# Group 13's block made in fp32 with the late groups, the last group's x and sums in other buffers, and new costs and preferences of the planner, in a causal attention and routed FFN kernel

## The chip, the cores and the metric

One core of one Trainium2 chip runs the whole program. The metric is the device time of one execution in microseconds (us). PE is TensorE, PEld its weight loads, ACT ScalarE, DVE VectorE, POOL GpSimd, SP the engine that issues all DMAs here.

## The reference

Input x is (2, 4096, 256) in fp32. Attention has one head of 256 channels and a causal mask; then a router takes the 3072 of 4096 rows with the highest score, and these alone go through a 256x256 block and a GELU.

```python
q, k, v = split(x @ w_attn + b_attn)
a = softmax(q @ k.T / 16 + causal_mask) @ v
x = layernorm(x + a @ w_proj + b_proj)
score = x @ w_router
top = top_k(score, 3072)                # in each batch of 4096 rows
y = x; y[top] = gelu(x[top] @ w_block)
out = layernorm(x + y)
```

## The kernel before

**Tiling.** Each batch of 4096 rows is cut into 8 groups of 512 queries: groups 0 to 7 and 8 to 15. A group of number g in its batch has 4(g+1) key tiles of 128 rows: four on the diagonal, the others in pairs. An fp32 product is made as three fp32r products of high and low parts (`split3`, L535), so all operands are split into a rounded copy (high) and a rest (low). Since w_proj is folded into the values, "sums" are what the reference has after w_proj. The last channel of the values is replaced by ones, so its sum is the softmax's denominator.

**Stages of a group.** Projection (`project`): x transposed is loaded, split (L821 to L839), and multiplied with A and WV into `fbank[0]`. First product (`scores`, L535 into `sbank`, two banks in turn): one tile is six matmuls; ACT copies it into `ring` (L955), 34 slots of 512 columns; the last two tiles of all go to `xraw`. DVE keeps a running maximum (`running`, L980 to L1001). `row_max`: four transposes (L1030), a reduction and two small steps (L1040 to L1047), four transposes back (L1053). `softmax`, for each diagonal tile or pair: DVE subtracts the maximum (L1066), ACT takes the exponential (L1073) and the high part (L1080, `parts`, three slots), DVE the low part (L1085). Second product (`values`, L1128 to L1136): six matmuls for a tile of up to 512 queries, into the two `obank` banks; its values come by DMA into `vs`, six slots. A slot of `ring` is free when its tile's second product is done, so at most four tiles of a group can still be open when the last tile of the last group but those in `xraw` is copied. For groups with g of 3 and more the sums come out turned: ACT (for the last group DVE, L1206) copies them into `ot_sb` (L1194), PE turns them back (L1225), DVE divides by the denominator and adds the residual (`evac`, L1240, L1244), then statistics (L1251, L1256), roots on POOL (`istd`, L1155 on), router sums on DVE (L1354, for the last group L1373) and normalised rows x1 on ACT (`norm`, L1343).

**x and its residual.** `attention_out` loads the group's x (L1177) into `xres[:, G % 2]`, POOL adds the bias (L1186). The load of group G waits until group G-2 has stored its x1, taken its router sums and made its y (`g_y`, which POOL's add at L1556 signals).

**The block.** Groups below `LATE` with g of 3 and more take an "upright" way: the block is applied to the turned sums plus scaled x columns (`rows_scale` L1446, `rows_add` L1452, high and low parts L1456 and L1460, 24 matmuls of 128x256 by `split3` into `fbank`, GELU L1477). x1 and y go to DRAM and come back for the end. Groups from `LATE` on (14 and 15 before) keep x1 and y in `tail`, at home(u, n), where they are wanted at the end: PE transposes x1 (`pe_t`, L1490), ACT copies it (`fhi`, L1502) to `late_x`, PE multiplies in plain fp32 (`pe_f`, L1524, two pieces of two matmuls for each half of a group, eight records to a half), ACT takes the GELU (L1542), POOL adds x1 (L1556) after the last router score, DVE takes statistics (L1562, L1567), POOL the roots (`late_own`, `late_sums`, L1788 to L1808). `tail` lies over `xT`, so a late group's norm waits for the last scores and the last projection. Banks of the late fills are listed in `bank_no`; `freed` gives what each waits for.

**Dummies.** `busy` (L593) issues matmuls without use; `late_busy` does so after certain late fills:

```python
def late_busy(pe):
    pe.wait_ge(v_h, QT * len(groups))
    busy(pe, fbank[2][:, :], 2)
# at the end of pe_t(pe, j):
if late and G + j > LATE:
    late_busy(pe)
```

v_h counts the tiles that `evac` has finished, 4 for each group.

**The end.** `search(1)` finds the threshold of the second batch in eight rounds: DVE compares (L1668), PE counts (L1724), DVE sums and decides (L1679, L1685). Then `ties`, sixteen picks on DVE (L1917) between rows scaled for either outcome (ACT, L1902 and L1907), and sixteen stores of 256 KB. Pairs of rows below the late groups are loaded during the last second product, paced with its loads of values (`paced`, L1850, L1851).

**The order.** All instructions lie in named streams for each engine (`at`). `merged` rehearses each (its waits gathered, its cost from `COSTS`), and `planned` simulates the engines and fixes one order for each, by the critical way that an operation has ahead of it (`urgency`) plus the preference of its stream (`PREFER_US`), after a time margin (`MARGIN_US`). On the chip each engine runs its order strictly, and so does SP with its DMAs.

## Time and profile before

| | us |
|---|---|
| median of 3 runs | 961.22 |
| the three runs | 964.9, 961.22, 958.93 |
| span of the profiled execution | 962.9 |
| PE busy | 934.3 (97%) |
| DVE busy | 791.0 (82%) |
| ACT busy | 637.6 (66%) |
| POOL busy | 303.6 (32%) |

The profiled execution's own time isn't given apart from its span; the span lies within the three times. Times in the rows are us from the span's start, durations of single instructions are ns where marked. An idle time in square brackets is the engine's just before the row, with what ended it. The end that the timeline gives a matmul is modelled: consecutive rows of 0.39 us start 0.23 us apart, and the chain of waits shows the 0.23.

### The profile page before, as it was taken

The page shows a single profiled execution, that of the slowest core. Times are in us where ns is not written, and L with a number is a line of the kernel's source. Part 1 is how long each engine was busy: PE and PEld are TensorE (multiplying, and loading weights), DVE is VectorE, ACT ScalarE, POOL GpSimd, SP SyncE. Part 2 cuts the span into 40 slices and gives each one's busy share as a digit, 9 for nine tenths or more (in the row PEclk, how much of TensorE's full clock was granted, in tenths as well). Part 3 has the DMA queues.
Part 4 walks back from the last instruction along what each step waited for, and adds up shares of the span by engine and source line. Part 5 has one row for each costly group of instructions (what it writes and reads, how often), then busy time and mean ns, then how long its engine had stood idle before and what let it go on. Part 6 is the DMA issues. An engine that isn't in the chain of part 4 may idle for free.

```text
span 962.9 us, 15643 instructions
## 1 busy us (share of the span) xinstructions
PE 934.3 (97%) x5018; PEld 799.2 (83%) x5018; DVE 791.0 (82%) x1494; ACT 637.6 (66%) x1009; POOL 303.6 (32%) x460
## 2 busy tenths in 40 slices
PE   9999999999999999999999999999999999998892
PEld 7889988888888888888889998888888888887671
DVE  5789886967976885699989898999899789489768
ACT  4467665764873776486757757586689577449794
POOL 3423231333220335414541253314212422131162
PEclk9999999999999999999999999999999999999996
DMA  6535344454364365488533633535769635347734
GB/s 212 166 114 171 113 141 122 120 158 126 101 184 116 102 187 155 132 255 277 175 109 94 199 108 110 164 102 172 247 223 295 212 106 153 99 144 241 264 128 175
DMA packets 89044, 155.84 MB, mean 162 GB/s; under 512 B 8442, under 2 KB 18300, under 8 KB 88964
## 3 DMA queue, kind: packets, MB, share of 16 engines
q1 hardware_dynamic: 88964, 154.85, 51.5%
q8 instruction: 41, 0.67, 0.3%
q14 instruction: 39, 0.32, 0.1%
HBM read 114.96 MB, written 39.86 MB: 161 GB/s over the span
## 4 chain that ended last, share of the span: by engine, by line
PE 93%; DVE 3%; DMA 1%; ACT 1%; issue 1%; DVEq 0%; POOL 0%; SPq 0%; ACTq 0%
PE sbank L535 38%; PE fbank L535 13%; PE obank L1134 11%; PE obank L1136 11%; PE obank L1135 10%; PE obank L1128 2%; PE obank L1130 2%; PE obank L1129 2%; DMA vs<-v_scratch 1%; PE fbank L1225 1%; PE mbank L1053 1%; PE mbank L1030 1%; DVE tail L1917 1%; PE fbank L1490 1%; DMA xraw<-xt 0%
## 5 line engine op out<-in xcount | busy, mean ns | idle before, releaser
L535 PE MATMUL sbank<-qT,xT 128*128 128x512 f32 (+2 forms) x1728 | 411.5, 378 | 0.2 <-issue 0.2
L535 PEld LDWEIGHTS sbank<-qT,xT 128*128 128x128 f32 x1728 | 304.9, 188 | 52.8 <-issue 0.6
L955 ACT COPY ring<-sbank 128x512 f32<-128x512 f32 (+3 forms) x286 | 156.2, 548 | 179.4 <-PE sbank L535 132.0
L1085 DVE TENSOR_TENSOR ring_lo<-ring,parts 128x1024 fp32r<-128x1024 f32 (+4 forms) x175 | 174.4, 1007 | 21.9 <-ACT parts L1080 21.3
L1134 PE MATMUL obank<-ring_lo,vs 128*128 128x512 f32 x476 | 182.5, 383 | 7.4 <-issue 3.5
L1136 PE MATMUL obank<-parts,vs 128*128 128x512 f32 x480 | 183.2, 382 | 0.0
L1135 PE MATMUL obank<-parts,vs 128*128 128x512 f32 x480 | 182.9, 381 | 0.0
L1080 ACT CAST parts<-ring 128x1024 fp32r<-128x1024 f32 (+4 forms) x175 | 144.8, 834 | 45.5 <-PE obank L1136 35.8
L1066 DVE TENSOR_TENSOR ring<-ring,mbank 128x1024 f32<-128x1024 f32 (+4 forms) x175 | 158.2, 944 | 7.3 <-PE mbank L1053 7.2
L1073 ACT ACTIVATE ring<-ring 128x1024 f32<-128x1024 f32 (+4 forms) x175 | 142.6, 842 | 21.6 <-DVE ring L1066 21.2
L997 DVE TENSOR_TENSOR runmax<-ring,runmax 128x1024 f32<-128x1024 f32 x84 | 106.6, 1269 | 59.3 <-ACT ring L955 58.6
L1134 PEld LDWEIGHTS obank<-ring_lo,vs 128*128 128x128 f32 x476 | 90.4, 190 | 25.1 <-issue 6.7
L1556 POOL TENSOR_TENSOR yb<-xres,yb 128x512 f32<-128x512 f32 x28 | 41.0, 1481 | 210.6 <-ACT yb L1542 80.1
L1136 PEld LDWEIGHTS obank<-parts,vs 128*128 128x128 f32 x480 | 90.9, 189 | 17.0
L1135 PEld LDWEIGHTS obank<-parts,vs 128*128 128x128 f32 x480 | 91.2, 190 | 16.1
L1186 POOL TENSOR_TENSOR xres<-xres,b_tot 128x512 f32<-128x512 f32 x32 | 49.0, 1554 | 67.5 <-DMA xres<-x 66.1
L839 POOL TENSOR_TENSOR xT<-xraw,xT 128x512 fp32r<-128x512 f32 x27 | 38.4, 1436 | 78.0 <-ACT xT L821 77.0
L1452 POOL TENSOR_TENSOR ot_sb<-ot_sb,yb 128x512 f32<-128x512 f32 x16 | 22.5, 1405 | 98.5 <-PE fbank L1225 80.6
L992 DVE TENSOR_TENSOR runmax<-ring,runmax 128x512 f32<-128x512 f32 (+3 forms) x74 | 44.9, 606 | 9.7 <-ACT ring L955 8.5
L535 PEld LDWEIGHTS fbank<-WV,xT 128*128 128x128 f32 x384 | 49.8, 191 | 2.3 <-issue 0.3
L535 PE MATMUL fbank<-WV,xT 128*128 128x256 f32 x384 | 51.2, 283 | 0.0
L535 PE MATMUL fbank<-xT,A 128*128 128x512 f32 x192 | 49.4, 393 | 0.2 <-POOL xT L839 0.2
(244 smaller groups left out, 1257.7 us busy)
## 6 DMA issues: line engine op xcount, KB each, us to landing
vs<-v_scratch SPq DMA_DIRECT2D x288, 256.0 KB, 2.9
v_scratch<-vnew SPq DMA_DIRECT2D x30, 512.0 KB, 3.1
xres<-x SPq DMA_DIRECT2D x16, 512.0 KB, 4.0
out<-tail SPq DMA_DIRECT2D x32, 256.0 KB, 2.8
x_scratch<-xres SPq DMA_DIRECT2D x14, 512.0 KB, 3.0
y_scratch<-yb SPq DMA_DIRECT2D x14, 512.0 KB, 4.1
tail<-x_scratch SPq DMA_DIRECT2D x28, 256.0 KB, 3.4
tail<-y_scratch SPq DMA_DIRECT2D x28, 256.0 KB, 4.0
```

The lines of the kernel that those rows point to most:

```text
L535: mm = eng.matmul(o, lhs(lh, k), rhs(rh, k), start=n == 0, stop=n == len(todo) - 1)
L955: act.copy(slot(n)[:, c0:], sbank[n % NSS][:, c0:]).then_inc(a_copy, 1)
L992: dve.tensor_tensor(runmax[:, 0, c0:], slot(n)[:, c0:], runmax[:, 0, c0:], ALU.max).then_inc(v_max, 1)
L997: dve.tensor_tensor(runmax[:, :, :], slots(ns, 0), runmax[:, :, :], ALU.max).then_inc(v_max, 1)
L1066: dve.tensor_tensor(slots(ns, c0), slots(ns, c0), mbank[:, None, c0:].broadcast_to([P, len(ns), GQ - c0]), ALU.subtract).then_inc(v_z, 1)
L1073: act.activation(slots(ns, c0), slots(ns, c0), ACT.Exp, scale=SCALE).then_inc(a_exp, 1)
L1080: act.copy(hi_of(u), slots(ns, c0)).then_inc(a_hi, 1)
L1085: dve.tensor_tensor(slots_lo(ns, c0), slots(ns, c0), f32(hi_of(u)), ALU.subtract).then_inc(v_lo, 1)
L1134: pe.matmul(o, vh, lo_, start=i == 0, stop=False)
L1135: pe.matmul(o, vh, hi_, start=False, stop=False)
L1136: mm = pe.matmul(o, vl, hi_, start=False, stop=last)
L1186: pool.tensor_tensor(r[:, 2 * j:2 * j + 2], r[:, 2 * j:2 * j + 2], b_tot[:, None, :].broadcast_to([P, 2, C]), ALU.add).then_inc(g_xres, 1)
```

## The change

`LATE` goes from 14 to 13, so group 13 takes the late way. With it `late_x` is laid out for up to eight halves of high parts, `bank_no` of the late fills has twelve entries (5 and 6 are `obank`, 3 and 4 `sbank`), and the wait of `pe_f` for the last group's first reciprocal holds for groups 14 and 15 alone. The last group's sums go to `sbank` (`summed`), so its second product waits for all score copies, and `obank` is free once group 14's sums are copied. The last group's x is loaded to its place in `tail`; the load waits for the last scores and projection. The router product of the last group goes to `mbank`. `block_sums` waits for `v_btot`, and each late group's roots for those of the late group before. The planner gets other costs, a model of a slowed PE after idle time, and new preferences and margins for nearly all streams.

```diff
-LATE = 2 * (T // GQ) - 2
+LATE = 2 * (T // GQ) - 3
+IDLE_US, SLOW_US = 1.3, 3.5
-PREFER_US = {"ffn flo": 100, "final load": 100, "project vhi": 100, "ffn store": 100, "last chain": 60,
...
+PREFER_US = {"final_roots own": 506, "project vhi": 455, "last": 412, "project qlo": 384, "scores copy": 369,
...
-MARGIN_US = {"attention_out router": 3, "final scale": 3, "project xhi": 2, "ffn flo": 2, "final_roots": 2,
...
+MARGIN_US = {"final own": 5, "attention_out norm": 5, "final sums": 3, "ffn sums": 3, "final_roots own": 3,
...
-COSTS = {"pe": (.0, 1 / 2400, .2), "act": (.13, 1 / 1200, .14), "dve": (.09, 1 / 960, .12),
-         "pool": (.35, 1 / 460, .1), "sp": (.45, 0.0, 0.0)}
+COSTS = {"pe": (.0, 1 / 2383, .2), "act": (.075, 1 / 1200, .17), "dve": (.065, 1 / 960, .13),
+         "pool": (.1, 1 / 445, .18), "sp": (.45, 0.0, 0.0)}
...
-        time = r.time * (COLD if n in COLD_STREAMS or e == "pe" and when < COLD_US else 1.0)
+        if e == "pe" and when > 2 * COLD_US and when - free[e] > IDLE_US:
+            slow = when + SLOW_US
+        time = r.time * (COLD if n in COLD_STREAMS or e == "pe" and when < slow else 1.0)
...
-        bank_no[f] = (3, 4, 5, 3, 4, 5, 6, 3)[4 * (G - LATE) + 2 * j + (kind == "ff")]
+        bank_no[f] = (5, 6, 5, 6, 5, 6, 5, 3, 4, 5, 6, 3)[4 * (G - LATE) + 2 * j + (kind == "ff")]
...
-                if bank_no[f] == 6:
-                    eng.wait_ge(v_ot, CC)
-                    eng.wait_ge(v_ow, 1)
-                elif bank_no[f] == 5:
-                    eng.wait_ge(v_ot, 1)
+                if bank_no[f] >= 5:
+                    eng.wait_ge(a_ot, CC * turned(len(groups) - 1))
                 elif bank_no[f] >= 3:
-                    eng.wait_ge(a_copy, n_tiles)
+                    eng.wait_ge(v_ot, bank_no[f] - 2)
...
-        last_ow = obank[1][:, 0:QT]
+        last_ow = mbank[:, 160:160 + QT]
+        summed = lambda G: sbank if G == len(groups) - 1 else obank
...
+                pe.wait_ge(v_btot, 1)
                 for k in range(CC):
...
-                    if G and straight(G - 1):
+                    if G == len(groups) - 1:
+                        pe.wait_ge(a_copy, n_tiles)
+                    elif G and straight(G - 1):
...
-                    o = obank[c][:, c0:]
+                    o = summed(G)[c][:, c0:]
...
+            if G == len(groups) - 1:
+                r = flat[:, (NUT - 2) * 512:NUT * 512].rearrange("p (t c) -> p t c", t=QT)
...
-                if G >= 2:
+                if G == len(groups) - 1:
+                    sp.wait_ge(p_s, n_tiles)
+                    filled(sp, ("v", G, 1))
+                elif G >= 2:
...
-                if late and 0 in tiles_:
+                if G >= len(groups) - 2 and 0 in tiles_:
                     pe.wait_ge(v_rs, 2 * len(groups) - 1)
...
-                    pool.wait_ge(g_own, 1)
+                if G > LATE:
+                    pool.wait_ge(g_own, G - LATE)
```

## Rows read from the trace of the kernel before

**Rows 1.** The page: busy time of each engine.
```profile
PE 934.3 (97%) x5018; PEld 799.2 (83%) x5018; DVE 791.0 (82%) x1494; ACT 637.6 (66%) x1009; POOL 303.6 (32%) x460
```

**Rows 2.** Busy time by stretch: length, PE, PEld, DVE, ACT, POOL, clock, DMA share, GB/s.
```profile
10.00:858.97 848.97, 847.92 (x4591) 732.51 (x4590) 704.80 (x1283) 559.11 (x879) 269.87 (x368) 1.00 0.51 157
858.97:869.81 10.84, 10.84 (x69) 9.43 (x67) 8.85 (x18) 4.98 (x10) 0.00 (x0) 1.00 0.64 197
869.81:923.97 54.16, 47.12 (x202) 38.47 (x203) 43.36 (x76) 45.11 (x65) 12.23 (x19) 0.94 0.79 267
923.97:931.34 7.37, 7.08 (x49) 5.97 (x48) 5.52 (x24) 7.04 (x14) 4.03 (x13) 1.00 0.00 1
931.34:949.35 18.01, 13.10 (x80) 7.76 (x78) 15.22 (x70) 16.50 (x38) 10.56 (x21) 0.90 0.01 1
949.35:962.90 13.55, 0.00 (x0) 0.00 (x0) 9.85 (x16) 2.08 (x4) 1.42 (x7) 0.50 0.83 310
...
870.00:880.00 10.00, 7.17 (x32) 6.16 (x33) 10.00 (x11) 9.98 (x13) 0.00 (x0) 0.88 0.63 226
```

**Rows 3.** Timeline of PE, 871 to 877: start, duration, instruction, idle before.
```profile
871.42 0.47 PE L1134 MATMUL obank<-ring_lo,vs 128*128 128x512 f32 x1 [1.61 <-ACT ot_sb L1194]
...
876.97 0.47 PE L1134 MATMUL obank<-ring_lo,vs 128*128 128x512 f32 x1 [1.41 <-ACT parts L1080]
```

**Rows 4.** Timeline of PE, 895 to 901.
```profile
895.18 0.47 PE L1134 MATMUL obank<-ring_lo,vs 128*128 128x512 f32 x1 [0.50 <-DMA vs<-v_scratch]
...
900.33 0.47 PE L1134 MATMUL obank<-ring_lo,vs 128*128 128x512 f32 x1 [3.52 <-issue]
```

**Rows 5.** The chain that ended last, 863 to 883: start, duration, what.
```profile
863.76 1.42 PE fbank L535 x12
...
870.21 1.06 ACT ot_sb L1194 x2
...
879.38 0.43 PE obank L1134
...
882.22 0.23 PE obank L1134
```

**Rows 6.** Timeline of DVE, 895 to 903.
```profile
895.77 1.49 DVE L1373 CUSTOM_DVE_ANT_0 runmax<-xres,wr 128x256 f32<-128x256 f32 x1 [4.25 <-POOL xres L1186]
...
897.44 0.43 DVE L1373 CUSTOM_DVE_ANT_0 runmax<-xres,wr 128x256 f32<-128x256 f32 x1 [0.17 <-DVE mcol L1373]
...
899.00 3.49 DVE L1085 TENSOR_TENSOR ring_lo<-ring,parts 128x1024 fp32r<-128x1024 f32 x3
```

**Rows 7.** Timeline of SP: the issue of the last load of x.
```profile
886.15 0.38 SPq L1177 DMA_DIRECT2D xres<-x  x1
```

**Rows 8.** Timeline of POOL, 881 to 897.
```profile
881.43 2.55 POOL L1556 TENSOR_TENSOR yb<-xres,yb 128x512 f32<-128x512 f32 x2 [22.62 <-issue]
894.45 2.53 POOL L1186 TENSOR_TENSOR xres<-xres,b_tot 128x512 f32<-128x512 f32 x2 [10.47 <-DMA xres<-x]
```

**Rows 9.** DMA queue, 894 to 898: packets, MB, share of the 16 engines.
```profile
q1 hardware_dynamic: 775, 1.41, 99.8%
```

**Rows 10.** Timeline of DVE, 860 to 862.
```profile
860.13 1.28 DVE L1460 TENSOR_TENSOR x1p<-ot_sb,vnew_b 128x512 fp32r<-128x512 f32 x2
```

**Rows 11.** Timeline of PE behind the last second product: fp32 blocks.
```profile
925.51 1.99 PE L1524 MATMUL sbank<-runmax,late_x 128*128 128x256 f32 x8
...
930.40 1.97 PE L1524 MATMUL sbank<-runmax,late_x 128*128 128x256 f32 x8 [0.29 <-issue]
```

**Rows 12.** Timeline of DVE, 932 to 940: count reductions, y statistics.
```profile
932.96 0.29 DVE L1679 TENSOR_REDUCE mbank<-fbank 128x15 f32<-128x120 f32 x1 [0.30 <-PE fbank L1724]
...
934.76 0.29 DVE L1679 TENSOR_REDUCE mbank<-fbank 128x15 f32<-128x120 f32 x1 [0.42 <-PE fbank L1724]
...
937.14 0.29 DVE L1679 TENSOR_REDUCE mbank<-fbank 128x15 f32<-128x120 f32 x1 [0.99 <-PE fbank L1724]
...
938.45 0.74 DVE L1562 BATCH_NORM_STATS2 bnst<-tail 128x6 f32<-128x256 f32 x2
```

48 lines of the change are left out of this document (30 added, 18 removed).

## The prediction

> **What bounds the kernel now.** I read the page first for the busy shares: PE is busy 934.3 us of the 962.9 us span [rows 1], so only what PE waits for, and what stands in front of it and behind it, can be won. Then I cut the span into stretches where the work changes [rows 2]. Of the 28.6 us in which PE idles, the stretches shown hold 26.8 us, so 1.8 us lie in the first 10. From 10 to 859 it idles 848.97 - 847.92 = 1.05 us in all, at full clock: a new order of instructions has next to nothing to win there and much to lose. From 859 to 869.8 (last scores, last row maxima, the held-back end of group 14's second product) it idles nothing. The second product of the last group, 869.8 to 924.0, holds PE busy for 47.1 of 54.2 us at a mean clock of 0.94: the 7.04 us idle and the slow clock are the loss to be had. From 924.0 to 931.3 the last chain makes the last scores of the router, from 931.3 to 949.4 DVE searches for the threshold, then sixteen picks and their stores follow, with DMA 0.83 busy. In these last three stretches PE isn't the bound; DVE is.
>
> The timeline of PE names the waits inside the product: 1.61 us for ACT's copy of group 14's sums, 1.41 us for the first pair's high parts [rows 3], 0.50 us for a load of values and 3.52 us put down to "issue" [rows 4]. Sum 7.04 us, all of the idle time. After the second and the fourth, the chain shows matmuls of 0.43 us in place of 0.23 [rows 5], eight each time, so 2 x 8 x 0.20 = 3.2 us more: the engine had been idle 3.0 us within 7 us, or 3.5 us at once, and the granted clock fell to 1.2 GHz. Loss in the product: 7.0 + 3.2 = 10.2 us.
>
> What is behind "issue"? DVE works in order. It stands 4.25 us in front of the last group's router sums (L1373), which wait for POOL's residual [rows 6], which starts at 894.45, 8.3 us after the load of x was issued at 886.15 [rows 7, 8]. The low parts that PE wants are queued behind at 899.00. And the load could go no earlier: it overwrites group 13's buffer, which POOL's add at L1556 reads until 884.0 [rows 8].
>
> **The change part by part.** The sum is made against the profiled execution: its span is 962.9 us; what lies around the span isn't shown, and the median of the runs is 961.2, so I take 1.7 us off at the end.
>
> Sums of the last group in sbank. The first values matmul of group 15 waits for its score copies (done before 860) and no longer for the ot copy. The 1.61 us wait goes. What is late next is ACT: it is busy 9.98 of the 10 us from 870 to 880 [rows 2], and the second wait (1.41 us) is for its high parts. But ACT's two ot copies (1.06 us on the chain [rows 5]) may now come after the exponentials, and with group 13's gelus late, four activations and two table loads leave that stretch of ACT. I expect both waits, 3.0 us, to shrink to about 1. Bounds: 0, and 3.0 if the idle time only moves from the first wait to the second.
>
> x of the last group in the tail. Its load now waits for the last scores and the last projection, both over by 860.5, not for 884.0. So x and the residual are there some 20 us before DVE asks. The 4.25 us wait of DVE goes and with it PE's 3.52 us. The four router sums (3.2 us of DVE, less with POOL gone) stay and have to lie where PE has low parts in stock. Bounds of the gain: 0 to 3.52 us, plus the clock; I take all.
> The price: the residual moves to where DVE makes the first low parts. The first router sum beside it took 1.49 us, its sisters 0.43 us [rows 6]. So two residual adds of 1.27 us can each hold up DVE by 1.1 us: 0 to 2.2 us, I take 0.5. That is a reason against the early x, in the same bounds.
>
> Loads. The product runs 0.79 of the DMA engines busy; between 894 and 898 they are at 99.8% [rows 9]. If PE waits less, the same values and paced loads are wanted in less time. Against that, group 13's x1 and y no longer go to DRAM and back, 2 MB, and its paced pairs are gone. I leave 1.0 us of waits for values (0.50 now; bounds 0 to 4). For the clock I leave 1.0 us of the 3.2, for a bout that is half as long.
> Left over in the product: 1.0 + 0.5 + 1.0 + 1.0 = 3.5 us. Gain: 10.2 - 3.5 = 6.7 us.
>
> Group 13's block in fp32. Out: 24 matmuls, 2 x 1.42 us [rows 5], at 863.8 to 868.4, and DVE's two low parts, 1.28 us, between the last maxima [rows 10]; rows, sums, their scaling and adding lie under PE's work and cost nothing. In: transposes 0.44 us and an fp32 block of 1.88 us for each half. Not all of it gets behind the second product, though. The second half's transposes end with late_busy, whose wait on v_h is for the last group's residual sums. One rehearsed operation takes all its waits together, and the real wait blocks what is queued behind. So only the first half (0.44 + 1.88 = 2.3 us) can be done behind the product, and the second half, with all of group 14, comes after 928. In 863 to 924 PE is relieved of 2.84 and given 2.3: gain 0.5 us. This holds if something covers the place from which 2.84 us go. PE has 6.9 us there (four held-back tiles of six matmuls of 0.23 us, and the last projection, twelve matmuls like those of 1.42 us [rows 5]), and the row maxima come 1.3 us or more earlier without the low parts, so the first values should be ready as the held-back ones end. If they aren't, up to 2.84 us of idle time appear: bound of loss.
>
> Behind the product. Before, group 14's first block (925.5) stood ahead of the router product, but DVE's own steps up to the aggregates last as long, so its going gives 0.1 us at most. After it PE made three more, the first at 930.4 [rows 11]; now it makes five, the first before the last score. One such block stretched a round of the search: reduction to reduction 2.38 us against 1.80, 0.6 us [rows 12]. Two more in this stretch, with their transposes: 1.0 us; bounds 0 (all of it in the gaps) and 4.6 us (all in the path). Two more pairs of y statistics on DVE (0.74 us each) fill the wait for a count, which is 0.42 us where nothing fills it [rows 12]: about 0.25 each, 0.5. POOL's two more adds (1.27 each) and one more chain of roots (eight small steps, by my estimate no longer than two such adds and a half) end before 958, when the pick of the last pairs needs them. Cost behind the product: 1.0 + 0.5 - 0.1 = 1.4 us.
>
> Planner's costs and preferences. They change the order of all five queues. Where PE idles 1.05 us in 849, I cost this at 0, with -1 as one end; the other end is open and is the third rival. The waits added at block_sums and in the roots of late groups lie on steps done long before: 0.
>
> Sum: 962.9 - 6.7 - 0.5 + 1.4 = 957.1 us of span, 955.4 us as a median.
>
> **The rivals.** (1) Nothing is left over in the product, and the new order hides the additional blocks: 962.9 - 10.2 - 0.5 + 0.3 = 952.5, with 1 us found in the head 951.5; median 949.8. For it: the waits have two named causes and both are cut; ACT and DVE have 9 and 11 us free in the product. Against: the first pair's way (exp, high, low) is serial, and DMA is near full.
> (2) The waits move. Loads of values now end the wait where x did (5.1 us kept), and 2.3 us of idle time open where group 13's block was cover: 962.9 - 10.2 + 5.1 + 2.3 + 1.4 = 961.5; median 959.8. For it: 99.8% DMA at the worst place; held-back values are limited to four tiles by the ring. Against: 2 MB less traffic.
> (3) Slower. The new order puts on DVE, in each group, an instruction that waits for a DMA or POOL ahead of the low parts, as L1373 did. The place is the second batch, where DVE is busiest. The price of one is that of 894 to 904: 3.52 + 1.6 = 5.1 us. From two such stalls on (10.2 against a gain of 5.8) the kernel is slower; with three it is 962.9 - 5.8 + 15.3 = 972.4, median 970.7. For it: such a stall is in the present order; large preferences overrule urgency. Against: only one in 963 us, and the present costs were cruder.
> (4) That the block isn't behind the product at all, its first half too coming after it: the 2.3 us change sides and the sum is within 1 us of the forecast.
>
> **How the numbers follow.** Forecast (with 4) 0.44, rival 1 0.26, rival 2 0.19, rival 3 0.11. About 1% (9.6 us) is what a measurement of this kernel tells from no change, as its three runs lie 6 us apart. Faster by over 1% means below 951.6: rival 1, 0.26. Slower by over 1%: rival 3 where it reaches three stalls, 0.10. Between: 0.64. The range of 8 in 10 runs from 948.5 (rival 1 with a little of the head) to 961.5 (rival 2 and a little more).
>
> **What would show it.** Right: no wait of PE for ot_sb; the load of x issued soon after 860, no DVE wait at the router sums; the product's stretch about 50 us (54.2 before) with under 3 us idle; one group of 8 fp32 matmuls for group 13 before the last values, the second after the last residual sums; five blocks behind; 18 to 19.5 us from last score to first pick. Wrong: PE idle between 20 and 859 of more than 2 us, or a product still as long with waits for vs, or a search of 21 us and more.

## The result, and the profile after

The changed kernel takes 977.46 us in the median of four runs (977.35 to 978.36); the kernel before, on the same chip, takes 962.55. The ratio is 1.0167, with a 95% interval of 1.0141 to 1.0194, all of it above 1: slower by 1.7%. The profiled run took 977.35 us with a span of 975.6, 12.7 us over the 962.9 of before. The prediction, 955.4 with a range up to 961.5, was wrong.

The stretches say where. These are the busy times of the changed kernel's stretches, in the columns of [rows 2], cut at the same events: start of the last second product (called "the product" from here on), its end, last score, first pick. The last row is a stretch of its own:
```profile
10.00:883.50 873.50, 859.44 (x4634) 739.30 (x4632) 707.36 (x1293) 552.49 (x879) 284.64 (x372) 1.00 0.48 153
883.50:929.94 46.44, 45.63 (x217) 38.09 (x217) 41.35 (x71) 46.37 (x71) 3.08 (x9) 1.00 0.84 284
929.94:937.28 7.34, 5.00 (x32) 3.57 (x31) 5.52 (x23) 7.32 (x15) 1.20 (x2) 0.76 0.00 0
937.28:962.13 24.85, 19.95 (x111) 13.65 (x109) 17.79 (x78) 14.98 (x31) 16.94 (x38) 0.91 0.00 1
962.13:975.60 13.47, 0.00 (x0) 0.00 (x0) 9.79 (x18) 3.97 (x8) 2.38 (x8) 0.50 0.84 311
...
700.00:800.00 100.00, 91.26 (x439) 74.80 (x438) 76.22 (x135) 61.76 (x101) 32.03 (x39) 0.98 0.64 208
```
Against [rows 2]: the product starts 883.5 - 869.8 = 13.7 us later; it is 54.2 - 46.4 = 7.7 us shorter; from its end to the first pick it is 32.2 against 25.4 us, 6.8 more; the picks take the same. 13.7 - 7.7 + 6.8 = 12.8, which is the difference.

**Ahead of the product.** From 10 us on PE idles 873.50 - 859.44 = 14.06 us there, where it had idled 1.05. 8.74 us of them lie between 700 and 800, the second batch, where the kernel before has PE busy for all of the 100 us. PE's timeline there has 0.55 + 2.46 + 1.35 = 4.4 us of waits for ACT's copies of scores, 2.42 for a row maximum of DVE, and 1.87 for POOL's xT. The timeline of ACT, 722 to 729, and under it that of PE, show how one of these waits comes about:
```profile
722.50 0.59 ACT L970 COPY ring<-sbank 128x512 f32<-128x512 f32 x1
726.23 1.09 ACT L1888 ACTIVATE tail<-tail,coef 128x256 f32<-128x256 f32 x2 [3.14 <-DMA tail<-y_scratch]
727.23 0.56 ACT L970 COPY ring<-sbank 128x512 f32<-128x512 f32 x1
...
722.36 3.03 PE L547 MATMUL sbank<-qT,xT 128*128 128x512 f32 x12 [0.55 <-ACT ring L970]
727.84 2.03 PE L547 MATMUL sbank<-qT,xT 128*128 128x512 f32 x6 [2.46 <-ACT ring L970]
729.67 0.63 PE L1151 MATMUL obank<-ring_lo,vs 128*128 128x512 f32 x1
```
ACT works in order. At 723.1 its next instruction is a scaling (L1888) of the first batch's final rows, work that nobody waits for soon; but its operand is still being loaded. The copy of scores (L970) that empties a bank for PE is queued behind it. ACT stands 3.14 us, PE 2.46, and the matmuls that follow take 0.63 us where their like took 0.39 just before: the granted clock went down to half. By groups of waits (total, times, longest), of the changed kernel and then of the kernel before:
```profile
ACT tail L1888 <- DMA tail<-y_scratch: 19.4, 6, 5.8
```
```profile
ACT tail L1907 <- DMA tail<-y_scratch: 1.1, 1, 1.1
ACT tail L1864 <- DMA tail<-y_scratch: 1.0, 1, 1.0
```

**In the product.** The load of x is issued at 877.17, 6.3 us ahead of the product's start (before, 886.15 [rows 7], 16.3 us behind it), and the residual is done before DVE asks; of PE's four waits [rows 3, 4] one of 0.81 us is left; the clock stays at 1.00. Timelines of SP, POOL and PE, and DVE's first router sum, which waits for nothing and takes 0.42 us in place of 1.49 [rows 6]:
```profile
877.17 0.38 SPq L1200 DMA_DIRECT2D tail<-x  x1
881.11 2.56 POOL L1209 TENSOR_TENSOR tail<-tail,b_tot 128x512 f32<-128x512 f32 x2 [42.17 <-DMA tail<-x]
884.31 0.47 PE L1151 MATMUL sbank<-ring_lo,vs 128*128 128x512 f32 x1 [0.81 <-ACT parts L1095]
913.83 0.42 DVE L1396 CUSTOM_DVE_ANT_0 runmax<-tail,wr 128x256 f32<-128x256 f32 x1
```

**Behind it.** The last score is there at 937.28. Timeline of PE, then DVE's first reductions of counts:
```profile
936.56 3.78 PE L1547 MATMUL obank<-runmax,late_x 128*128 128x256 f32 x8 [1.38 <-ACT late_x L1525]
941.65 0.22 PE L1747 MATMUL fbank<-cmp,ones_bf 128*128 128x120 bf16 x1
...
941.90 0.29 DVE L1702 TENSOR_REDUCE mbank<-fbank 128x15 f32<-128x120 f32 x1 [2.31 <-PE fbank L1747]
944.79 0.26 DVE L1702 TENSOR_REDUCE mbank<-fbank 128x15 f32<-128x120 f32 x1
```
The fp32 block of group 13's second half comes at 936.56, after the last residual sums, and at half clock: 3.78 us where [rows 11] have 1.97. The first count's matmul stands behind it, and behind the dummies and the four transposes of the next half, so the first reduction comes 4.6 us after the last score, where before it came 1.6 us after it (932.96 [rows 12] against 931.34).

PE's order sets these 3.0 us, since the comparison that the count wants is done at 939.30. A smaller delay stands behind it. Ahead of the comparison DVE turns the scores into keys, an operation of 128x8. In the changed kernel POOL's first addition of y, which waited for the last score, runs beside it; before, none did. Timelines of POOL and DVE in the changed kernel, and of DVE before:
```profile
937.43 1.26 POOL L1579 TENSOR_TENSOR tail<-tail 128x512 f32<-128x512 f32 x1 [1.04 <-DVE score L1415]
937.72 1.00 DVE L1668 TENSOR_SCALAR keyi<-keyi 128x8 uint32<-128x8 uint32 x1
```
```profile
931.82 0.17 DVE L1645 TENSOR_SCALAR keyi<-keyi 128x8 uint32<-128x8 uint32 x1
```
DVE takes 1.00 us for eight columns, where it took 0.17, and is done as POOL's addition ends. It takes 0.96 to 1.00 us in all fourteen kernels of this document where such an addition runs beside it, and 0.17 in the three where none does (before, e3_buffers, e13_before_tuned). As long as PE is late this costs nothing more; with PE out of the way it does (e8_countfirst below).

From the first of the eight reductions to the last it takes 17.4 us instead of 14.0 (941.90 to 959.33; 932.96 to 947.00).

### The profile page after: what moved, and what is told of

It is laid out like the page before. It is cut to its first block, busy times and chain, and to the rows that moved or that the text cites. A ratio compares the mean times of both kernels' runs of the same rounds, so it can differ in the third digit from the quotient of the medians.

```text
span 975.6 us, 15627 instructions
## 1 busy us (share of the span) xinstructions
PE 938.8 (96%) x5022; PEld 800.2 (82%) x5022; DVE 784.7 (80%) x1490; ACT 628.1 (64%) x1003; POOL 313.7 (32%) x462
## 4 chain that ended last, share of the span: by engine, by line
PE 76%; issue 6%; DVE 6%; DMA 5%; POOL 3%; ACT 2%; SPq 1%; DVEq 0%; ACTq 0%; POOLq 0%
PE sbank L547 31%; PE fbank L547 10%; PE obank L1151 8%; PE obank L1153 8%; PE obank L1152 8%; DMA out<-tail 2%; PE obank L1145 1%; PE obank L1146 1%; PE obank L1147 1%; PE sbank L1151 1%; PE sbank L1153 1%; PE sbank L1152 1%; DVE ring_lo L1100 1%; DMA tail<-y_scratch 1%; DMA ring<-xt 1%
## 5 line engine op out<-in xcount | busy, mean ns | idle before, releaser
L970 ACT COPY ring<-sbank 128x512 f32<-128x512 f32 (+3 forms) x286 | 157.1, 551 | 174.9 <-PE sbank L547 122.8
L1151 PE MATMUL obank<-ring_lo,vs 128*128 128x512 f32 (+3 forms) x416 | 159.1, 382 | 0.8 <-ACT parts L1095 0.8
L1153 PE MATMUL obank<-parts,vs 128*128 128x512 f32 (+3 forms) x416 | 157.8, 379 | 0.0
L1152 PE MATMUL obank<-parts,vs 128*128 128x512 f32 (+3 forms) x416 | 157.7, 379 | 0.0
L1153 PEld LDWEIGHTS obank<-parts,vs 128*128 128x128 f32 x416 | 78.5, 189 | 14.7
L1151 PEld LDWEIGHTS obank<-ring_lo,vs 128*128 128x128 f32 x416 | 78.6, 189 | 14.5 <-ACT parts L1095 1.0
L1152 PEld LDWEIGHTS obank<-parts,vs 128*128 128x128 f32 x416 | 78.6, 189 | 13.5
L1475 POOL TENSOR_TENSOR ot_sb<-ot_sb,yb 128x512 f32<-128x512 f32 x14 | 24.9, 1782 | 160.8 <-DVE yb L1469 150.6
L854 POOL TENSOR_TENSOR xT<-xraw,xT 128x512 fp32r<-128x512 f32 x27 | 40.5, 1515 | 66.6 <-ACT xT L836 65.7
L1209 POOL TENSOR_TENSOR xres<-xres,b_tot 128x512 f32<-128x512 f32 x30 | 44.8, 1518 | 51.9 <-DMA xres<-x 50.6
L1579 POOL TENSOR_TENSOR yb<-xres,yb 128x512 f32<-128x512 f32 x26 | 37.5, 1460 | 60.3 <-ACT yb L1565 27.6
L1172 POOL TENSOR_SCALAR roots<-mv_h 128x4 f32<-128x4 f32 x15 | 7.8, 519 | 151.3 <-DVE mv_h L1279 125.8
```

The lines of the kernel that those rows point to most:

```text
L854: pool.tensor_tensor(xT[:, 1, k, cols], raw_of(G)[:, k, :], f32(xT[:, 0, k, cols]), ALU.subtract).then_inc(g_xlo, 1)
L970: act.copy(slot(n)[:, c0:], sbank[n % NSS][:, c0:]).then_inc(a_copy, 1)
L1151: pe.matmul(o, vh, lo_, start=i == 0, stop=False)
L1152: pe.matmul(o, vh, hi_, start=False, stop=False)
L1153: mm = pe.matmul(o, vl, hi_, start=False, stop=last)
L1209: pool.tensor_tensor(r[:, 2 * j:2 * j + 2], r[:, 2 * j:2 * j + 2], b_tot[:, None, :].broadcast_to([P, 2, C]), ALU.add).then_inc(g_xres, 1)
```

## Experiments

Each time stands against runs of the kernel before on the same chip (medians 961.45, 960.48, 960.90, 961.47 and 961.01 for the five sets below). "Idle ahead" is PE's from 10 us to the start of the last product.

**1. Orders and structure apart.** e1_newplan is the kernel before with the changed planner alone: its costs, its idle rule, and its PREFER_US and MARGIN_US.
```
+IDLE_US, SLOW_US = 1.3, 3.5
...
-COSTS = {"pe": (.0, 1 / 2400, .2), "act": (.13, 1 / 1200, .14), "dve": (.09, 1 / 960, .12),
-         "pool": (.35, 1 / 460, .1), "sp": (.45, 0.0, 0.0)}
+COSTS = {"pe": (.0, 1 / 2383, .2), "act": (.075, 1 / 1200, .17), "dve": (.065, 1 / 960, .13),
+         "pool": (.1, 1 / 445, .18), "sp": (.45, 0.0, 0.0)}
```

> The kernel before with the planner's new costs, model, preferences and margins alone. Theory (the new order makes the loss): PE idles 8 us or more between 10 and the start of the last product (1.05 before, 14.1 in the changed kernel), and the time is 970 to 977. Rival (the late form of group 13 and the new buffers make it, the order only follows them): under 3 us idle there, 958 to 964.

Measured: 990.46 us, ratio 1.0303 (1.0285 to 1.032), 13 us above even the range of the theory. The planner's numbers alone cost 29 us, and the buffers have no part in it:
```profile
10.00:888.80 878.80, 867.29 (x4658) 747.28 (x4656) 717.00 (x1305) 557.90 (x888) 289.24 (x380) 0.99 0.50 155
```
11.5 us idle ahead, and a start 19 us late. From the product's end (942.12) to the first pick (974.20) it takes 32.1 us, 6.7 more than before, without any additional block there.

e2_oldplan is the reverse: the changed kernel with COSTS, PREFER_US and MARGIN_US of before, and without the new idle rule. e3_buffers is the buffers alone, with the block left early and the old planner:
```
-LATE = 2 * (T // GQ) - 3
+LATE = 2 * (T // GQ) - 2
```

> The changed kernel with the planner's old costs, preferences and margins. Theory (order): under 3 us idle before the last product, the product shorter by 6 to 8 us than before, the stretch behind it longer by 2 to 7, so 955 to 963. Rival (structure): 8 us or more idle, 970 and more.

> The old plan and only two late groups, but the last group's sums and x in the other buffers. Theory (the product's gain comes from the early x and the early start, the loss behind it from group 13's two more blocks): the wait of 3.5 us and that of 1.6 us are gone, the stretch behind the product stays at 39 us, 953 to 957. Rival (the gain hangs on the new order): the product keeps its 54 us, 960 to 963.

Measured: e2_oldplan 976.60 us, 1.0153 (1.0135 to 1.017); e3_buffers 981.78, 1.0212 (1.0192 to 1.0232). Both miss the theory's ranges, 955 to 963 and 953 to 957; e2_oldplan has the rival's time (970 and more) without its 8 us of idle time, and e3_buffers lies above its rival's 960 to 963 too. Ahead of the product, first e2_oldplan, then e3_buffers:
```profile
10.00:871.30 861.30, 857.69 (x4637) 740.84 (x4635) 707.20 (x1266) 559.04 (x877) 264.20 (x356) 1.00 0.50 155
```
```profile
10.00:867.00 857.00, 855.59 (x4635) 739.27 (x4633) 708.79 (x1270) 558.81 (x876) 266.76 (x356) 1.00 0.50 157
```
The middle is nearly whole again (3.6 us idle in e2_oldplan, 1.4 in e3_buffers). The product is no shorter than before: 55.4 us in e2_oldplan, and 55.3 in e3_buffers, whose last matmul of it ends at 922.3, with the early block's 24 matmuls inside it; PE then waits 5.1 us until DVE copies the last sums at 929.30. PE, DVE and ACT of e2_oldplan:
```profile
873.69 0.67 PE L1136 MATMUL sbank<-ring_lo,vs 128*128 128x512 f32 x1 [2.43 <-issue]
884.10 0.76 PE L1136 MATMUL sbank<-ring_lo,vs 128*128 128x512 f32 x1 [4.84 <-ACT parts L1080]
...
871.04 1.47 DVE L1381 CUSTOM_DVE_ANT_0 runmax<-tail,wr 128x256 f32<-128x256 f32 x1 [1.32 <-POOL tail L1194]
...
877.65 1.09 ACT L1916 ACTIVATE tail<-tail,fin 128x256 f32<-128x256 f32 x2 [0.77 <-DMA tail<-y_scratch]
```
The old preferences, with x there early, put a router sum in front of the first low part: that is the way to the wait of 2.43 us. The larger one, 4.84, has nothing to do with x: ACT makes four scalings of final rows, from 877.65 on, ahead of the first pair's exponential, and DVE five subtractions ahead of its low part. So the early x buys nothing by itself; it needs an order that puts its readers, and the scalings, later. The four kernels stand at 961.5 (before, old planner), 990.5 (before, new), 976.6 (changed, old) and 977.5 (changed, new): each half of the change loses with the other half missing, and the two together lose as well. The 1.47 us beside POOL's residual are [rows 6]' 1.49 once more.

Most of what these two lose lies behind the product: 5.1 us more to the first pick in e2_oldplan and 14.1 in e3_buffers, and in both 4.5 more in the picks, 18.0 us against 13.5 (e7_oldpref_dma28 and e10_gate below have the same). There DVE takes the last statistics of y only behind fourteen picks, and the last two picks then wait for POOL's roots and ACT's scalings; of e2_oldplan:
```profile
970.95 0.73 DVE L1926 COPY_PREDICATED tail<-mbank,tail 128x512 f32<-128x512 uint32 x1 [4.31 <-ACT tail L1916]
```

**2. The scalings in the middle.** e4_scale_margin is the changed kernel with one number changed, so that the planner keeps a scaling back until 3 us after its operand is due:
```
-             "final scale": 0.3, "ffn flo": 0.3, "proj": 0.3, "scores": 0.3, "ffn fhi": 0.3}
+             "final scale": 3, "ffn flo": 0.3, "proj": 0.3, "scores": 0.3, "ffn fhi": 0.3}
```

> The changed kernel with the margin of the stream final scale back at 3 us (0.3 in the change). Theory (ACT stands in front of the first batch's scalings, whose rows haven't landed, with score copies queued behind): the 14.7 us that ACT waits for tail between 700 and 800 shrink under 4, PE's 8.7 us idle there shrink under 3, and the time is 966 to 970. Rival (PE is starved there by the whole order, and the waits are slack): 975 to 979.

Measured: 972.01 us, 1.0135 (1.0091 to 1.0178).
```profile
700.00:800.00 100.00, 96.32 (x484) 80.79 (x483) 80.98 (x141) 68.23 (x114) 34.74 (x40) 1.00 0.68 220
ACT tail L1888 <- DMA tail<-y_scratch: 9.5, 5, 4.1
```
ACT's waits for these loads are halved, PE's idle time from 700 to 800 falls from 8.74 to 3.68 us, and 5.4 us of the time go: the mechanism is shown, as one cause of several (9.6 us idle ahead are left). The theory had expected more of it: waits under 4 us, PE's idle time under 3, and 966 to 970 us.

e6_dma28 (the changed kernel, planner's latency of a transfer 2.8 us instead of 2.0) and e7_oldpref_dma28 (that, with the preferences and margins of before) ask whether the planner just believes in too quick a load:
```
-DMA_US, DMA_BYTES_US, FIRST_BYTES_US = 2.0, 320e3, 250e3
+DMA_US, DMA_BYTES_US, FIRST_BYTES_US = 2.8, 320e3, 250e3
```

> The changed kernel, with one number of the planner different: a DMA's latency is taken as 2.8 us in place of 2.0. Theory (the new order was fitted so closely to 2.0 us that loads which land later hold up engines in order): PE's 14.1 us idle before the last product fall to 6 to 11, the last product's end moves forward by 3 to 8 us, and the time is 970 to 975, even though the preferences were chosen for the other number. Rival (loads aren't what delays; a wrong latency only makes the order worse): 977 to 990.

> The changed kernel with the old preferences and margins, the new costs and the latency of 2.8 us. Theory (preferences chosen with the wrong latency make the loss before the product): under 4 us of PE idle before the last product, its end at 916 to 921, and 966 to 972 in all. Rival (the new preferences are right and the costs are what matters): no better than 974.

Measured: 975.34 us, 1.0156 (1.0134 to 1.0179), with 13.0 us idle ahead, where the theory had 6 to 11: with the new preferences the latency is at most a small part of the cause. e7_oldpref_dma28: 973.23, 1.0135 (1.0119 to 1.015), 4.5 us ahead, 51.5 in the product. From 700 to 800 PE is busy for 94.2 us in e6_dma28, and in e7_oldpref_dma28:
```profile
700.00:800.00 100.00, 99.70 (x507) 84.84 (x507) 89.09 (x157) 75.65 (x124) 26.53 (x40) 1.00 0.56 187
```
The preferences and margins make the holes. e7_oldpref_dma28 was expected at 966 to 972. It missed that by its product, which kept only 2.7 of the 7.7 us, and by its picks, 18.0 us.

**3. The 6.8 us behind the product.** e5_tailcut keeps the changed kernel's order and computes only 16 of the 256 columns of the blocks (13, 1) and (14, 0) (the other columns are left out):
```
+                    cut = 16 if EMIT and (G, j) in ((LATE, 1), (LATE + 1, 0)) else C
...
-                        mm = pe.matmul(bank_of(("ff", G, j))[:, t * C:(t + 1) * C],
-                                       x1p_of(G, j)[:, 0, k * 2 * P + t * P:k * 2 * P + (t + 1) * P], late_wb[:, k],
+                        mm = pe.matmul(bank_of(("ff", G, j))[:, t * C:t * C + cut],
+                                       x1p_of(G, j)[:, 0, k * 2 * P + t * P:k * 2 * P + (t + 1) * P],
+                                       late_wb[:, k, 0:cut],
```
EMIT is set once the order is planned.

> The changed kernel in its own order on every engine, but the fp32 block of group 13's second half and that of group 14's first half compute 16 of 256 columns. Theory (these two blocks, newly behind the product, lie in the path of the search): the 24.9 us between the last score and the first pick shrink by 3 to 6 us, and the time is 972 to 975. Rival (the search waits for statistics, roots and copies on DVE, POOL and ACT, and PE's blocks lie in its gaps): under 1 us, 976.5 to 978. Either way the stretches up to the end of the last product stay as they are.

Measured: 978.79 us, 1.0188 (1.0171 to 1.0205). Last score to first pick: 24.15 us, 0.7 less. The theory, which had 3 to 6 us, falls. The first of the two blocks got 1.9 us shorter (1.89 for 3.78), but the first reduction comes only 0.7 us nearer to the last score (3.9 us after it): the transposes behind the block still run at half clock here, 1.06 us against 0.60 in the changed kernel. The stretch's clock is 0.85 against 0.91, so this run says what less work on PE is worth with the slower clock that came with it. The time is above both ranges because the product also starts 5.4 us later (last section).

e8_countfirst moves two instructions, e9_ownroots takes POOL's load off (the own scales of groups 14 and 15 are left out):
```
+for e, what, ahead in (("pe", ("last", 1), ("late", 6)), ("act", ("ffn fhi", 27), ("final sums", 17))):
+    orders[e].remove(what)
+    orders[e].insert(orders[e].index(ahead), what)
```
```
+if not (EMIT and G > LATE):
     link(pool, pool.tensor_tensor(tmp[:, 0], mv_h[:, b, tiles_, 1], rs, ALU.mult))
...
```

> The changed kernel in full, with two instructions moved in the planner's order: the first count of the second search (product L1747) ahead of the transposes and dummies of tile pair (14, 0), and ScalarE's copy of late_x (L1525) for the block (13, 1) ahead of the last three scalings L1931 of that place. In the changed kernel the first reduction of counts comes 4.6 us after the last score, though the comparison for it is done 2.2 us earlier. Theory A (the order of PE ahead of the first count sets the 24.85 us from last score to first pick): the first reduction at 2.3 to 2.6 us, first pick 1.8 to 2.3 us earlier, time 975 to 975.7 against 977.5. Theory B (GpSimd sets it: it has no gap from 944.97 to 961.9, three additions of y L1579 and four sets of roots L1812 to L1832, and the last stats and the last roots stand behind them): the first reduction moves, the first pick by under 0.7 us, time 976.8 to 977.8.

> The changed kernel's own order, but seven of the eight instructions of the own roots (L1812 to L1818) are left out for groups 14 and 15, so that the scales of those rows' own halves are not computed. GpSimd stands at them from 949.11 to 955.0, between two additions of y. Theory A (PE's order ahead of the first count): the time stays within 0.5 us. Theory B (GpSimd's chain): the additions of 955.16 come 4 to 5.5 us earlier, VectorE's wait of 0.99 us at 956.45 goes, its stats of y move up into earlier rounds, the last scales L1832 come 4 to 5 us before 965.3, and the first pick comes 1 to 2.5 us earlier: time 975 to 976.5.

Measured: e8_countfirst 976.69 us, 1.016 (1.0134 to 1.0186), 23.5 us from last score to first pick; e9_ownroots 977.86, 1.0173 (1.0149 to 1.0197), 23.1 us. DVE's first reductions in e8_countfirst:
```profile
939.31 0.29 DVE L1705 TENSOR_REDUCE mbank<-fbank 128x15 f32<-128x120 f32 x1 [0.29 <-PE fbank L1750]
943.51 0.29 DVE L1705 TENSOR_REDUCE mbank<-fbank 128x15 f32<-128x120 f32 x1 [1.23 <-PE fbank L1750]
```
In e8_countfirst the first reduction comes 2.6 us after the last score, as theory A had it (1.6 before; the rest is mostly the 0.83 us of the keys), but the second comes 4.2 us after the first (2.9 in the changed kernel): the transposes and dummies have only moved behind the first count, and group 14's first block stands between the matmuls of the second, as in the changed kernel, but later. 1.3 us of the stretch are won, the time falls by 0.8, between the two theories. In e9_ownroots 14 instructions of POOL are gone, and POOL now waits for ACT's gelus instead (2.79 us before its addition at 961.90); of its 1.75 us at most 0.7 are POOL's (954.08 to 957.12, 3.0 us for that round in the changed kernel, and 2.4 here), the rest is the first count, earlier under a better clock (its first reduction comes 3.5 us after the score). The time didn't fall (977.86), which is what theory A had, not B's 975 to 976.5; the profiled run here is a long one (last section). Neither theory is the cause alone: what is behind the product is a chain through all four engines, and taking weight from one of them shifts the wait to the next.

e10_gate is e7_oldpref_dma28 with the dummies that wait for the last scores kept away from groups 13 and 14:
```
-if late and G + j > LATE:
+if late and G + j > len(groups) - 2:
     late_busy(pe)
...
-if G == LATE and j:
+if G == len(groups) - 2 and j:
     late_busy(pe)
```

> As e7_oldpref_dma28 (the changed structure, the preferences and margins of before, new costs, 2.8 us for a transfer), but the dummies that wait for the last scores (late_busy) stand only behind the tile pairs of the last two pairs, not behind those of groups 13 and 14, so that the transposes and blocks of group 13 and of 14's first half need not follow the last residual sums. Theory: that wait is why only one of six blocks lies inside the second product; without it three or four lie there, the stretch from product's end to last score stays 7.3 to 8.5 us, last score to first pick falls from 22.9 to 19 to 21 us, and the time from 973.2 to 970 to 972. Rival (vector and GpSimd work behind the blocks sets that stretch, whichever blocks are done): 972.7 to 974.

Measured: 972.82 us, 1.0118 (1.0096 to 1.0139), against 973.23. Product's end to last score, and last score to first pick, in e7_oldpref_dma28 and in e10_gate:
```profile
924.08:931.43 7.35, 6.57 (x41) 5.40 (x39) 5.53 (x24) 3.68 (x9) 1.20 (x2) 0.84 0.01 2
931.43:954.36 22.93, 18.04 (x105) 11.51 (x103) 17.90 (x70) 14.62 (x31) 16.98 (x38) 0.95 0.00 1
```
```profile
924.04:933.19 9.15, 8.81 (x58) 7.71 (x59) 5.53 (x24) 4.70 (x10) 1.20 (x2) 1.00 0.00 0
933.19:953.29 20.10, 13.80 (x80) 7.70 (x78) 17.50 (x70) 12.28 (x25) 15.06 (x34) 0.93 0.00 1
```
The blocks that no longer wait for the scores lie ahead of them and delay them by 1.8 us; the search gets shorter by 2.8. 1.0 us is left of it in the span, and 0.4 in the time, which is within what runs differ by, as the rival had it.

**4. What the structure is worth with an order made for it.** e11_tuned and e12_tuned_gate (changed structure, the latter with e10_gate's dummies) and e13_before_tuned (structure of before) each have PREFER_US and MARGIN_US chosen anew, some 60 numbers each. Of e12_tuned_gate the shortest part of the edit:
```
-DMA_US, DMA_BYTES_US, FIRST_BYTES_US = 2.0, 320e3, 250e3
+DMA_US, DMA_BYTES_US, FIRST_BYTES_US = 3.6, 320e3, 250e3
...
-        delay = DMA_US + r.bytes / DMA_BYTES_US if e == "sp" else r.delay
+        delay = 2.8 + r.bytes / DMA_BYTES_US if e == "sp" else r.delay
```

> The changed kernel in full (both buffers, the third block late), with another set of PREFER_US and MARGIN_US and 2.8 us for a transfer, chosen so that the order loses little when a transfer takes 2 or 4.5 us. Theory (the order, not the buffers, costs the 13 us ahead of the last product): PE idle from 10 us to the product under 3 us, product start at 868 to 872, product 46 to 50 us, the stretch behind it to the first pick 28 to 32 us; time 956 to 963. Rival (the structure itself costs something in the middle or the stretch behind cannot shrink): idle over 4 us or a time of 968 and more, as with e7_oldpref_dma28 and e10_gate.

> As e11_tuned, with dummies that wait for the last scores only behind the tile pairs of the last two pairs (as in e10_gate), its own preferences and margins, and 3.6 us for a transfer in the order (2.8 in the urgencies). By the theory two or more blocks lie within the second product; time 956 to 963, and last score to first pick 17.5 to 20.5 us. By the rival 968 and more.

> The kernel before (its buffers, group 13's block early) with the new costs and preferences and margins chosen in the same way. This is the other side of the comparison: what the change of buffers and block is worth with an order made for each. If the product's gain (7 to 8 us) survives the cost behind it (4 to 7), e11_tuned is 1 to 4 us under this one. Theory: 958 to 961.5 here. Rival (buffers worth nothing once the order is right): this one is not slower than e11_tuned and e12_tuned_gate by over 1 us.

Measured: 967.85 us, 1.0062 (1.0047 to 1.0077); 965.34, 1.0048 (1.0034 to 1.0061); 972.27, 1.0116 (1.0102 to 1.0129). Ahead of the product, in this order:
```profile
10.00:874.55 864.55, 859.39 (x4636) 740.55 (x4634) 705.60 (x1279) 556.90 (x882) 271.75 (x356) 1.00 0.49 155
```
```profile
10.00:873.22 863.22, 859.07 (x4634) 739.67 (x4632) 705.85 (x1279) 556.05 (x882) 275.83 (x356) 1.00 0.49 155
```
```profile
10.00:878.14 868.14, 860.85 (x4657) 741.20 (x4655) 712.50 (x1301) 558.62 (x888) 291.97 (x368) 1.00 0.49 156
```
5.2, 4.2 and 7.3 us idle: none gets back to the 1.05 us of the old order. From product's start to first pick the three take 78.2, 77.7 and 78.3 us (before 79.5). e11_tuned and e12_tuned_gate lie between theory and rival, e13_before_tuned far outside its 958 to 961.5. With orders made in the same way the changed structure is 4 to 7 us ahead, nearly all of it ahead of the product. That is one order for each; for the kernel before such an order came out 11 us worse than its old one, so 4 to 7 us don't show what the structure is worth. What separates all three from 961.5 is still the middle.

e14_head and e15_head_gate take the middle as it was: the instructions of all five queues in the order of the kernel before, written out up to 830 us of the planner's time, and the planner behind that.
```
+    heads = {e: head_of(e) for e in todo}
...
+                head = heads[e][len(orders[e])] if len(orders[e]) < len(heads[e]) else n
-                if place[e][n] < len(ops):
+                if place[e][n] < len(ops) and n == head:
```

> The changed kernel in full, its instructions ordered exactly as in the kernel before on all five queues up to 830 us of the planner's time (692 of PE's steps, 947 of VectorE's; what the changed kernel no longer has is left out of the list), and by the planner behind that, with preferences chosen for the rest. Theory (the 13.7 us ahead of the last product are the order's alone): PE idle from 10 us to the product under 1.5 us, product start 868.5 to 870.5, product and stretch behind to the first pick 76 to 79 us together (before 79.5, after 78.6, e12_tuned_gate 77.7), time 955 to 960. Rival (the changed buffers themselves cost something ahead of the product, as all kernels with them idled 3.6 us and more there, e3_buffers alone excepted): idle 3 us and more, time 963 and more.

> As e14_head, with dummies that wait for the last scores only behind the tile pairs of the last two pairs, and its own preferences behind the first 830 us of planner's time. Theory as for e14_head, with the last score to the first pick at 17 to 20 us instead of 20 to 25 and a longer product: time 955 to 960. If the wait in those dummies costs something that the order can't hide, this one is 1 us and more below e14_head; if not, they are within 1 us.

Measured: e14_head 958.93 us, ratio 0.9973 (0.9956 to 0.999); e15_head_gate 957.61, 0.9971 (0.9958 to 0.9984), both a little below the kernel before and far below the changed one, and both within the 955 to 960 expected. e14_head, and then e15_head_gate with its product and the stretch from last score to first pick:
```profile
10.00:867.30 857.30, 856.09 (x4636) 739.17 (x4634) 711.82 (x1293) 562.45 (x884) 268.78 (x372) 1.00 0.50 156
...
921.68:945.66 23.98, 19.74 (x109) 13.84 (x107) 17.99 (x77) 14.38 (x29) 16.50 (x35) 0.86 0.00 1
```
```profile
10.00:867.05 857.05, 855.98 (x4635) 739.11 (x4633) 707.14 (x1293) 562.13 (x884) 269.03 (x371) 1.00 0.50 156
867.05:913.36 46.31, 45.21 (x213) 37.30 (x213) 42.54 (x71) 44.78 (x69) 5.65 (x10) 1.00 0.85 285
...
921.23:942.14 20.91, 16.43 (x97) 10.65 (x97) 18.70 (x78) 11.36 (x24) 14.65 (x31) 0.98 0.00 1
```
Idle ahead is 1.2 and 1.1 us, the start comes at 867.3 and 867.05, and 869.81 - 867.05 = 2.8 us is just what group 13's early block had held of PE (2 x 1.42 [rows 5]). The changed buffers cost nothing ahead of the product. The dummies' wait: the clock from last score to first pick is 0.86 with it and 0.98 without, the stretch 24.0 and 20.9 us, and the medians are 1.3 us apart, though their intervals overlap. The two also have different preferences behind 830 us, so the difference isn't shown to be the dummies' alone. The 20.9 us are just above the 17 to 20 expected.

The residual lies beside the first low parts in both, as the prediction had it. POOL's timeline, DVE's low parts (L1173: shortest, median and longest in ns) and PE's first wait in the product, all of e14_head; then DVE's timeline in the changed kernel, where the subtractions lie beside the residual (881.11, above) and the low parts all but behind it:
```profile
865.79 2.54 POOL L1282 TENSOR_TENSOR tail<-tail,b_tot 128x512 f32<-128x512 f32 x2 [11.31 <-DMA tail<-x]
L1173 DVE TENSOR_TENSOR ring_lo<-ring,parts x3: 410/545/1560, 867.3 to 869.3; 128x512 fp32r<-128x512 f32 x1, 128x384 fp32r<-128x384 f32 x1, 128x256 fp32r<-128x256 f32 x1
868.98 0.47 PE L1224 MATMUL sbank<-ring_lo,vs 128*128 128x512 f32 x1 [1.68 <-ACT parts L1168]
```
```profile
880.79 2.81 DVE L1081 TENSOR_TENSOR ring<-ring,mbank 128x512 f32<-128x512 f32 x5 [0.75 <-PE mbank L1068]
883.52 1.16 DVE L1100 TENSOR_TENSOR ring_lo<-ring,parts 128x512 fp32r<-128x512 f32 x2
```
The first low part, 128x512, takes 1.56 us beside the residual and 0.69 in the changed kernel, and PE waits 1.68 us in place of 0.81: its row names ACT's high parts, but they end at 866.6 and the low part at 868.9. In e15_head_gate the first low part takes 0.84 us and PE waits 0.96; the second, 128x384, takes 1.64 in place of 0.55 and holds nobody up. The subtractions read mbank, which is in PSUM: though four of the five lie wholly beside POOL's additions in the changed kernel, they take 2.81 us, the same as in the kernel before (865.65), where POOL does nothing at that time.

## Why the prediction was wrong

**The step that failed** is "They change the order of all five queues. Where PE idles 1.05 us in 849, I cost this at 0, with -1 as one end; the other end is open and is the third rival." It measured: product start 13.7 us later instead of 0. Against e15_head_gate, same structure and the old order ahead of the product, it is 883.5 - 867.05 = 16.5 us: 13.0 of PE idle time; for the other 3.5 I can point to slow matmuls only, as behind 727.84. A row of the kernel before shows what its order achieves, and nothing of how narrow that is. The warning was there: the first paragraph reads the 1.05 us as "next to nothing to win there and much to lose", and the sum then takes 0 for it. Every other order that ran was worse: 3.7 to 16.8 us of idle time ahead with the new costs, 1.4 and 3.6 with the old ones and the changed structure.

**Rival 3** named the way: an instruction that waits for a DMA, in the second batch, in front of what PE wants. Its engine was off (ACT's scalings, not DVE), its price per stall too (5.1 us; the largest was 2.5 us of idle time, with the slower clock behind it). Its three stalls gave 970.7; the median was 977.46. 0.11 was too small a chance for a case whose other end I had called open.

**The product: the mechanism right, the gain forecast too low.** The forecast of 6.7 + 0.5 = 7.2 us is for 863 to 924, where 2.84 us go ahead of the product and 2.3 come into it; for the product alone it comes to 54.2 - 6.7 + 2.3 = 49.8 us ("about 50"). Measured: 46.4. The waits for the ot copy, for x and for values are gone, one of 0.81 us is left, the clock is 1.00 throughout. Of the 3.5 us left over in the sum, the loads (1.0), the slower clock (1.0) and the residual (0.5) came to nothing; DMA at 0.84 busy held nobody up. Of the 3.4 us of difference these three are 2.5 and the first waits 0.2 (0.81 for 1.0); 0.7 I can't put to a term. The residual cost nothing because this order has the router sums 30 us behind it and the low parts starting as it ends (883.52). Where it lies beside the first low part, the term is real: in e14_head PE waits 0.9 us more there, within the 0 to 2.2 of the prediction. In e2_oldplan the router sum beside it takes 1.47 us, its sisters 0.41. The Trainium skill (SBUF — State Buffer, "Who interferes with whom") says that a DVE operation with two SBUF inputs and a GpSimd one that reads SBUF contend, and that DVE operations with one SBUF input outside the fast modes don't; the trace agrees, with the low parts slowed and the subtractions from mbank not.

But e2_oldplan and e3_buffers show that the gain isn't the buffers' own. I took it as their property ("Its load now waits for the last scores"); with the old preferences the product takes 55.4 and 55.3 us. The gain belongs to buffers and order together.

**Behind the product: the mechanism right, the size wrong.** That only the first half of the block can lie in the product, and the second comes after the last residual sums, was right (889.50 and 936.56). "Cost behind the product: 1.0 + 0.5 - 0.1 = 1.4 us" measured 6.8, above the bound of 4.6 for the blocks, and "18 to 19.5 us from last score to first pick" measured 24.85. I priced two more blocks in the search's rounds at 1.0 us together, from the 0.6 us of one in [rows 12]. I hadn't asked what stands ahead of the first count: there the block took 3.78 us, since PE had just waited and its clock was at half, with dummies and transposes behind it. That is 3.0 of the 6.8 us (first reduction 4.6 us after the score against 1.6), of which e8_countfirst won back 2.0 and then stood at the keys' 0.83; 3.4 lie in the rounds: four statistics of y in one of them (2.9 us), blocks in others, one wait for POOL; 0.4 lies between the last reduction and the first pick. e5_tailcut, e8_countfirst and e9_ownroots each took one of these weights off and won 0.7 to 1.75 us of the stretch; of the times only e8_countfirst's fell, by 0.8 us. And not all of the 6.8 us is the block's: e1_newplan, with the same preferences and no late block of group 13, loses 6.7 us there, while e15_head_gate, with the block late and another order, loses 3.4.

**What the change is worth.** With the order of before kept ahead of the product, the changed structure gives 0.9973 (e14_head) and, with the dummies also changed, 0.9971 (e15_head_gate, 957.6 us). That isn't the prediction come true, since these are other kernels than the one predicted. The stretches of e15_head_gate against [rows 2]: 2.8 us won ahead of the product, 7.9 in it, and 3.4 lost behind it (28.8 against 25.4), 7.2 of span; of the medians it is 3.4 us (957.6 against 961.0), as the profiled run of before was one of its longer ones. Both kernels also have preferences newly chosen for what comes behind 830 us, and no run gives the kernel before the same; so the 3.4 us aren't shown to be the structure's own. What is shown is that the buffers cost nothing ahead of the product: the changed kernel lost there by the order that came with them.

What stays open: which of the preferences makes which hole. Only the scalings' margin and the latency of a transfer were tried alone; and PE's idle time up to 660 us, 6.6 us against 2.8 before, has no experiment of its own. Nor has POOL's addition beside the keys; a kernel that only makes it later would be one.

## What to carry to other kernels

Where one engine is busy all but 1 us in 850, any change that reorders the queues is a change to that stretch, and its cost has to be bounded from above before anything else: change structure under a fixed order first (or fix the old order up to the place changed), and only then let the planner loose. Work that nobody waits for soon, but that waits for a load, is dangerous on an in-order engine that also empties the busiest engine's banks. A gain made by earlier data counts only with an order that doesn't put its readers in front of what the busiest engine wants.

## What the runs showed of the hardware that I had not expected

The start of the kernel has more than one outcome for the same order. e5_tailcut has the changed kernel's order there, yet its last product starts 5.4 us later. PE's wait for ACT's copy and the stretch from 20 to 25 us, in the changed kernel and in e5_tailcut:
```profile
17.25 0.98 PE L547 MATMUL sbank<-qT,xT 128*128 128x256 f32 x6 [0.86 <-ACT ring L970]
20.00:25.00 5.00, 5.00 (x35) 4.59 (x34) 2.37 (x8) 1.86 (x3) 0.00 (x0) 1.00 0.29 108
```
```profile
18.10 1.30 PE L548 MATMUL sbank<-qT,xT 128*128 128x256 f32 x6 [1.50 <-ACT ring L971]
20.00:25.00 5.00, 5.00 (x18) 3.65 (x17) 1.68 (x6) 0.00 (x0) 0.00 (x0) 0.50 0.02 5
```
PE is busy for all 5 us in both, but with 35 matmuls in one and 18 in the other. Where the wait was 0.86 us, the granted clock stayed at 1.00; where it was 1.50 (2.01 in e9_ownroots, 2.06 in e1_newplan), it fell to 0.50, the lower level, and in these 5 us ACT did little or nothing (0 to 0.37 us) and DMA moved next to nothing, which I can't explain. The profiled run of e9_ownroots is such a one: 984.93 us, where the median of the kernel is 977.86. A wait at the start that is 0.6 to 1.2 us longer goes with a product that starts 5.4 (e5_tailcut) and 7.9 us later (e9_ownroots); that all of this comes from the wait isn't shown. Part of e1_newplan's 19 us is probably of this kind (its clock from 20 to 40 us is 0.81).
